# A GNN kernel's edge loop: block words loaded in the sixth step of a turn, with the addresses and waits of the next 27 matmuls computed ahead of the load

## The reference

```python
N, E, D, EF, L = (3125, 12500, 128, 16, 3)        # the inputs have 100,000 edges
s2, d2 = concatenate([src, dst]), concatenate([dst, src])
for l in range(L):
    e_in = concatenate([h_prev[s2], h_prev[d2], ef2], axis=-1)
    msg = leaky_relu(e_in @ We1[l]) @ We2[l]
    red = segment_sum(msg, d2, num_segments=N)
    n_in = concatenate([h_prev, red], axis=-1)
    out = leaky_relu(n_in @ Wn1[l]) @ Wn2[l]
    h_prev = out + h_prev
x = layernorm(x + out)
```

## The kernel before

| ahead of | step 0 | steps 1 and 2 | steps 3 to 11, each |
|---|---|---|---|
| tile 1 | 5 (38) | 3 (15) | 3 (15) |
| tile 2 | 3 (15) | 3 (15) | 3 (15) |
| tile 3 | 3 (13) | 3 (13) | 3 (13) |
| sums | 6 (33) | 6 (33) | 2 (12) |

## Time and profile before

### The profile page before, as it was taken

The page is one execution under the profiler, slowest core; times in us unless marked ns, Lnnn a source line. Parts: engine busy times, 40 slices in busy tenths (PEclk is TensorE's granted clock), DMA queues, the critical chain, the costliest instruction groups (busy, mean ns, idle before and its releaser), DMA issues.

```text
span 4538.9 us, 95215 instructions
## 1 busy us (share of the span) xinstructions
PE 3134.0 (69%) x28957; PEld 2255.1 (50%) x28958; DVE 2927.2 (64%) x7075; ACT 2092.5 (46%) x4052; POOL 780.5 (17%) x826
## 2 busy tenths in 40 slices
PE   3443443443442558888888879898888788988886
PEld 2111111111110556666666657777777577767774
DVE  7444444444443369999999966666666566666665
ACT  0000000000000346666666667777777677777774
POOL 0455555555555100000000000000000000000000
PEclk6555555555555779999999989999999899999998
DMA  6000000000000646666565624444444244444443
GB/s 176 4 5 5 5 5 5 5 5 5 5 5 5 147 123 212 207 213 209 207 215 204 214 102 162 162 154 163 153 159 157 86 164 152 164 152 159 157 155 112
DMA packets 191495, 533.07 MB, mean 117 GB/s; under 512 B 34359, under 2 KB 71958, under 8 KB 189430
## 3 DMA queue, kind: packets, MB, share of 16 engines
q1 hardware_dynamic: 163926, 517.51, 34.1%
q0 software_dynamic: 27552, 15.37, 1.8%
HBM read 375.40 MB, written 157.52 MB: 117 GB/s over the span
## 4 chain that ended last, share of the span: by engine, by line
PE 46%; DVE 10%; issue 9%; DMA 2%; ACT 1%; POOL 0%; DVEq 0%; SPq 0%; ACTq 0%; POOLq 0%
PE gath L1096 16%; PE sums L1151 12%; PE sums L1096 8%; PE gath L1089 5%; DVE loop_buf L875 3%; DVE loop_buf L892 2%; DVE big L806 2%; PE sums L1089 2%; DMA recc<-records 2%; PE sums L1001 1%; DVE gsel L810 1%; PE sums L1159 0%; PE sums L1021 0%; PE sums L1160 0%; PE sums L1165 0%
## 5 line engine op out<-in xcount | busy, mean ns | idle before, releaser
L806 DVE SCALAR_TENSOR_TENSOR big<-big 128x768 f32<-128x768 f32 (+1 forms) x957 | 907.7, 949 | 676.4 <-ACT big L593 635.0
L1096 PE MATMUL gath<-t_hi,gsel 128*128 x3744 | 944.9, 278 | 0.0
L1096 PE MATMUL gath<-t_lo,gsel 128*128 x3744 | 944.3, 278 | 0.0
L1151 PE MATMUL sums<-loop_buf 128*128 128x128 f16 x11232 | 793.7, 221 | 202.6 <-issue 202.0
L875 DVE TENSOR_TENSOR loop_buf<-big,loop_buf 128x768 f16<-128x768 f32 x936 | 889.7, 951 | 0.0
L507 POOL DMA_INDIRECT records<-rec,rowi x784 | 754.7, 963 | 630.7 <-DVE rec L747 391.2
L984 PE MATMUL sums<-t_lo,tri 128*128 128x326 f16 x784 | 345.5, 454 | 714.0 <-issue 480.2
L1151 PEld LDWEIGHTS sums<-loop_buf 128*128 128x128 f16 x11232 | 680.7, 99 | 311.0 <-issue 156.8
L725 DVE SCALAR_TENSOR_TENSOR gsel<-sums,t_lo 128x326 f32<-128x326 f32 x784 | 367.3, 496 | 724.0 <-remote 536.6
L597 ACT ACTIVATE loop_buf<-big 128x768 f16<-128x768 f32 x936 | 782.0, 836 | 1.9
L593 ACT ACTIVATE big<-gath 128x512 f32<-128x512 f32 x936 | 559.6, 598 | 356.8 <-PE gath L1096 356.8
(11 more groups left out here) (156 smaller groups left out, 2632.1 us busy)
## 6 DMA issues: line engine op xcount, KB each, us to landing
gsel<-gsel_d SPq DMA_DIRECT2D x208, 576.0 KB, 3.9
loop_buf<-ssel_d SPq DMA_DIRECT2D x208, 576.0 KB, 5.1
numb<-nums_d SPq DMA_DIRECT2D x106, 576.0 KB, 4.6
gsel_d<-gsel SPq DMA_DIRECT2D x104, 576.0 KB, 5.5
ssel_d<-loop_buf SPq DMA_DIRECT2D x104, 576.0 KB, 6.5
fchunk<-feat_d SPq DMA_DIRECT2D x313, 144.0 KB, 2.9
records<-rec,rowi POOLq DMA_INDIRECT x784
recc<-records POOLq DMA_DIRECT2D x30, 272.0 KB, 5.1
```

The source lines that it names most:

```text
L806: return dve.scalar_tensor_tensor(m, m, SLOPE, m, ALU.mult, ALU.max)
L1096: return pe.matmul(uv, gsel[:, h, (2 * tc + s) * P:(2 * tc + s + 1) * P], at[n], start=False, stop=n == 3, skip_group_check=True)
L1151: last = pe.matmul(out_n, m[:, place, w0:w0 + D], ssel[:, ts, s, :], start=False, stop=False, skip_group_check=True)
```

## The change

The load goes from the last step of a turn to the sixth (`q == LOAD_AT - 1`, `LOAD_AT` = 6). It now loads 16 words, those of steps 3 to 18 counted from the start of this turn, so up to step 6 of the next turn. Steps 0 to 5, and the gathers of step 6, use what the turn before has loaded; the rest of step 6 to step 11 uses what this turn loads. The load ahead of the loop fills the last ten registers. Each step takes its words with a snap of its own where it needs them (`word_of` is now a function), one for the gathers and one for the sums, instead of one snap of every register at the head of the turn. In step 5, ahead of the load, the addresses of its own 12 sum matmuls and the addresses and wait values of the 15 gather and feature matmuls of step 6 are worked out (`StepValues`), so that 27 matmuls can be issued behind the load with no register work between them. Matmuls, waits, operands and the other engines are unchanged.

```diff
--- before.py
+++ after.py
@@ -60,7 +60,9 @@
 BANK = 512
 BANKS = -(-NODES // BANK)
 AHEAD = 1
-WORDS = STEPS + LAG
+LOAD_AT = STEPS // 2
+WORDS = STEPS + LAG + 1
+FIRST_WORD = LOAD_AT - LAG
 BLOCK_BITS = 5
 assert NB <= 1 << BLOCK_BITS and STEP * 2 * BLOCK_BITS < 32
 SLOPE = 0.01
@@ -1037,17 +1039,19 @@
 
                     pe.reg_load(words, map_row[0:1, ds(first, WORDS)])
 
-                load_words(0)
+                pe.reg_load(words[STEPS - FIRST_WORD - LAG:], map_row[0:1, 0:WORDS - (STEPS - FIRST_WORD - LAG)])
                 with nc.Fori(0, TURNS, engines=(mybir.EngineType.PE,), hint_back_edge=True) as it:
                     with pe.If(it < live_n):
-                        word_of = [pe.snap(r) for r in words]
                         step0 = pe.snap(l * live_n * STEPS + it * STEPS)
                         turn = pe.snap((l * live_n + it) * PER_TURN)
 
-                        def places(t):
-
-                            q, i = divmod(t, STEP)
-                            word, nodes = word_of[q + LAG], []
+                        def word_of(step, before_load):
+
+                            return pe.snap(words[step - FIRST_WORD + (STEPS if before_load else 0)])
+
+                        def places(word, i):
+
+                            nodes = []
                             for k in (2 * i, 2 * i + 1):
                                 field = word // (1 << k * BLOCK_BITS) if k else word
                                 if k + 1 < 2 * STEP:
@@ -1061,17 +1065,17 @@
 
                             return t[:, plane * NODES:(plane + 2) * NODES].rearrange("p (k n) -> p k n", k=2)[:, :, ds(node0, P)]
 
-                        def gather_rows(t):
-
-                            lo, hi = places(t)
+                        def gather_rows(word, i):
+
+                            lo, hi = places(word, i)
                             at = rows(t_hi, lo, 0), rows(t_lo, lo, 0), rows(t_hi, hi, 1), rows(t_lo, hi, 1)
                             for ap in at:
                                 pe.lower_ap(ap)
                             return at
 
-                        def sum_places(t):
-
-                            lo, hi = places(t)
+                        def sum_places(word, i):
+
+                            lo, hi = places(word, i)
                             at = sums[:, ds(lo, P)], sums[:, ds(hi, P)]
                             for ap in at:
                                 pe.lower_ap(ap)
@@ -1096,6 +1100,26 @@
                             return pe.matmul(uv, gsel[:, h, (2 * tc + s) * P:(2 * tc + s + 1) * P], at[n], start=False,
                                              stop=n == 3, skip_group_check=True)
 
+                        class StepValues:
+
+                            def __init__(self, q):
+
+                                self.q = q
+                                self.word = word_of(q, q <= LOAD_AT)
+
+                            def tile(self, i):
+
+                                return gather_rows(self.word, i)
+
+                            def waits(self):
+
+                                q = self.q
+                                self.part_in = at_least(turn + upto(q // PART_STEPS)) if q % PART_STEPS == 0 else None
+                                self.x_free = at_least(step0 + (q + AHEAD))
+                                self.free6 = at_least(step0 + (q + 1))
+                                self.lo_in = at_least(step0 + (q + LO_AHEAD - LAG + 2))
+
+                        ready = None
                         for q in range(STEPS):
                             p = q // PART_STEPS
                             h = p % 2
@@ -1104,46 +1128,49 @@
                             uv6, uv7 = gath6, (gath[:, 0:2 * D], gath[:, 2 * D:4 * D])
 
 
-                            rows0 = gather_rows(t)
+                            now, rows_of = ready or (StepValues(q), None)
+                            if ready is None:
+                                now.waits()
+                            rows0 = rows_of[0] if rows_of else now.tile(0)
                             if first:
-                                part_in = at_least(turn + upto(p))
-                            x_free = at_least(step0 + (q + AHEAD))
-                            if first:
-                                pe.wait_ge(fchunk_in[h], part_in)
+                                pe.wait_ge(fchunk_in[h], now.part_in)
                             features(uv6, t, h, False)
                             if first:
-                                pe.wait_ge(gsel_set[h], part_in)
+                                pe.wait_ge(gsel_set[h], now.part_in)
                             for n in range(4):
                                 last = gather(uv6, rows0, t, h, n)
                             last.then_inc(gath6_done, 1)
 
 
-                            rows1 = gather_rows(t + 1)
-                            pe.wait_ge(x_set, x_free)
+                            rows1 = rows_of[1] if rows_of else now.tile(1)
+                            pe.wait_ge(x_set, now.x_free)
                             features(uv7[0], t + 1, h, True)
                             for n in range(4):
                                 gather(uv7[0], rows1, t + 1, h, n)
 
 
-                            rows2 = gather_rows(t + 2)
-                            free6 = at_least(step0 + (q + 1))
-                            lo_in = at_least(step0 + (q + LO_AHEAD - LAG + 2))
+                            rows2 = rows_of[2] if rows_of else now.tile(2)
                             if first:
-                                pe.wait_ge(ssel_set[1 - h], part_in)
+                                pe.wait_ge(ssel_set[1 - h], now.part_in)
                             features(uv7[1], t + 2, h, True)
-                            pe.wait_ge(mlo_set, lo_in)
+                            pe.wait_ge(mlo_set, now.lo_in)
                             for n in range(4):
                                 last = gather(uv7[1], rows2, t + 2, h, n)
                             last.then_inc(gath7_done, 1)
 
 
+                            of_sums = word_of(q - LAG, q < LOAD_AT)
+                            sum_at = [sum_places(of_sums, i) for i in range(STEP)]
+                            ready = None
+                            if q == LOAD_AT - 1:
+                                after = StepValues(q + 1)
+                                after.waits()
+                                ready = after, [after.tile(i) for i in range(STEP)]
+                                load_words(it * STEPS + FIRST_WORD + LAG)
+                            pe.wait_ge(gath6_free, now.free6)
                             place = (q - LAG) % RING
-                            sum_at = {t + i - STEP * LAG: sum_places(t + i - STEP * LAG) for i in range(STEP)}
-                            if q == STEPS - 1:
-                                load_words((it + 1) * STEPS)
-                            pe.wait_ge(gath6_free, free6)
                             for i in range(STEP):
-                                at_lo, at_hi = sum_at[t + i - STEP * LAG]
+                                at_lo, at_hi = sum_at[i]
                                 ts = (t + i - STEP * LAG) % SLOTS
                                 for s, out_n in ((1, at_hi), (0, at_lo)):
                                     w0 = i * 2 * D + (1 - s) * D
```

## The result

| | kernel before | kernel after |
|---|---|---|
| median (lowest to highest), us | 4537.26 (4534.35 to 4543.8) | 5414.4 (5409.38 to 5416.34) |
| profiled execution, its span, us | 4540.7, 4538.9 | 5413.0, 5411.3 |
| turn in pass 1 / 2 / 3, us | 36.58 / 33.63 / 33.67 | 47.82 / 44.87 / 44.96 |
| granted clock over the span | 0.806 | 0.792 |

The ratio of the times is 1.193, 95% interval 1.191 to 1.195: +877 us where +530 was forecast, and 234 us above the upper end of the range. A turn is here the mean distance of the first matmuls of step 0 of consecutive turns, over the 26 turns of a pass. The growth of the turns, 26 x 11.24 + 52 x 11.27, is 878 us, so practically all of it lies in the edge loop.

A forecast was written before the change was run, and what follows sets the result against it. PE's sequencer, working out addresses in registers, was taken as the bound nearly everywhere (DVE in pass 1). Turns of 41.3 us in passes 2 and 3 and 41.5 in pass 1 add 530 us: forecast 5067 us, range 4990 to 5180.

The forecast's parts named there:

- Unit price: Price of one register instruction on PE's sequencer, read at three places of the trace: 0.214 us.
- Words where they are used, +7.7 us a turn: Steps 3 to 11: sums' addresses worked out anew, 6 register instructions instead of 2, +7.7 us a turn.
- The rival of shared snaps: Builder shares equal snaps, so steps 3, 4, 5, 10, 11 keep 2 instructions; 4732 us, chance 0.05.
- Snaps, 0: Head of turn: 15 snaps go, 24 single ones come; between -0.4 and +0.4 us a turn, taken as 0.
- addresses ahead of the load, 0: Step 5: addresses and waits of 27 matmuls worked out before the load, same instructions in another order, price 0.
- back edge, 0: End of turn: branches stay, PE's gap shrinks but the sequencer's 2.0 us do not; price 0.
- The load's 1.5 us stay: Load moved from step 11 to step 5 still costs 1.5 us a turn; 16th word adds 0 to +0.1.
- The clock, 0 to +0.5: After the load, idle PE may drop to 1.2 GHz for the 27 matmuls: 0 to +0.5 us, caught up by step 9.
- Pass 1 at 41.5: Pass 1: PE becomes later than DVE, whose bursts hold it up a little; 41.5 us a turn, between 40.8 and 43.2.
- the sequencer has no lead: Rejects the faster rival: sequencer runs ahead of PE, hiding the load in passes 2 and 3; 4397 us, chance 0.05.
- the clock did not stay low: Rejects the rival that PE stays at 1.2 GHz, 56 us a turn; 6214 us, chance 0.03.
- the change did what it says: Rejects the no-change rival: extra addresses cancel against something in the order, within 0.2%; 4537 us, chance 0.01.

The follow-up runs named there:

- e12: Kernel after, but in steps 3, 4, 5, 9, 10 and 11 the sums reuse the word kept from the gathers three steps earlier; 4695.41 us (kernel before beside it 4194.14).
- e1: Kernel before with words taken by a snap of their own where used; load stays in step 11 with 15 words; 4813.51 us (kernel before beside it 4196.88).
- e2: Kernel after without the load in the loop, registers filled once ahead of a pass, most blocks wrong; 4611.89 us (kernel before beside it 4196.88).
- e10: Kernel before with a 16th word loaded into a spare register from the same place; 4150.23 us (kernel before beside it 4194.14).
- e9: Kernel before, its 15-word load beginning at 12 x turn + 6, blocks wrong; 4379.79 us (kernel before beside it 4194.14).
- e11: Kernel after, its load beginning at 12 x turn + 4 instead of + 6, blocks wrong; 4837.6 us (kernel before beside it 4194.14).
- e18: Kernel after with one-hot stores of pass 1 and their loads in passes 2 and 3 cut to one partition of 128; 5363.39 us (kernel before beside it 4564.57).
- v2: Kernel before with a 16-word load and fields cut by one remainder; 4034.76 us (kernel before beside it 4196.65), ratio 0.962.
- e6: Kernel after with the load put ahead of 13 of the 14 register instructions in step 5; 5419.81 us (kernel before beside it 4543.55).
- e8: Kernel after with the load behind the 6 register instructions for step 5's sums, ahead of the other 8; 5430.9 us (kernel before beside it 4543.55).
- e14: Kernel after with the load in the seventh step, first word 12 x turn + 7, ahead of the addresses; 5056.49 us (kernel before beside it 4196.65).
- e13: Kernel after with the load in the fourth step, first word 12 x turn + 4, blocks right; 4754.59 us (kernel before beside it 4196.65).
- e3: Kernel before without the load in the loop, four words used over and over, blocks wrong; 4073.51 us (kernel before beside it 4196.88).

## Why the prediction was wrong, point by point

- *What bounds the kernel* was right. Unit price: 0.214 us was read from before; e12's 24 instructions gave 0.21 each, after's 14 a step (the prediction counted 15) 3.15/14 = 0.225.
- *Words where they are used, +7.7 us a turn*: right. Steps of 3.21 were forecast, 3.15 came; e1, with this part alone, has turns of 41.76 in pass 2, +8.1, of which 0.3 is the load's. The rival of shared snaps was wrong; the sharing has to be written by hand (e12).
- *Snaps, 0*, *addresses ahead of the load, 0*, *back edge, 0*: the sum was right and its parts were not. After without the load (e2) has the turn forecast for it, 39.84 against 39.8. But the sums of steps 5, 6 and 7 come 4.67, 3.30 and 2.83 us apart, 10.8 for three steps that would take 9.4 at 3.12: computing ahead costs 1.4 us, since only part of what step 5 spends more comes back. The way from the sums of step 11 to those of step 1 is 7.19 and not 7.80, and the other steps' 3.12 for 3.21 make up the rest.
- ***The load's 1.5 us stay*: this step failed.** It carried a price measured at one place to another. I changed the words from 15 to 16 and the first word from 12 x turn to 12 x turn + 6 on paper, and priced only the first (+0.1; it is -0.5 by e10). The place costs 2.0 us for 15 words (e9 against before), 2.7 for 16 (after against e11). The hold was 4.0 us and not 1.5, each with the instruction for the load's address. By the Trainium skill (Runtime: NRT & Kernel Launch, Instruction fetch mechanics) a load takes about 200 ns a register even in bulk, an estimate of 3.2 us for 16. I had set it aside because before's 15 words took 1.5. It is near to what the misplaced load shows, 0.25 a word, and three times the 1.0 us of the aligned one (e10). The page's figure and the row differed by half, and I took the row as the truth of every load instead of asking what made it cheap.
- *The clock, 0 to +0.5*: at its upper end or above. PE stood still for 6 us, the 12 sums behind it took 1.46 us (1.2 GHz), and the turn is 5.03 us longer than without the load, of which 4.02 is the hold. The other 1.0 us is spread behind it, 0.75 of it in step 6 (4.05 against e2's 3.30), so that the term was about twice what I allowed.
- *Pass 1 at 41.5*: wrong on top, 47.82. Besides the 5.0 us, 2.6 come from the stores of one-hots that are issued just ahead of the load there (e18). The forecast looked at the queue of SP only for waits, and the load's new time had not been laid beside the transfers'.
- *The sum*: 52 x (44.9 - 41.3) + 26 x (47.8 - 41.5) = 351 us, which is the 347 between the forecast and the median. Of these some 195 are the load's hold (2.5 x 78 turns), some 80 what follows the low clock, and some 70 the stores in pass 1.
- *The rivals*: the sequencer has no lead (without its load, before's step 11 falls to the 2.35 of its neighbours, and the holds of 1 to 15 accesses show on PE in proportion), the clock did not stay low, and the change did what it says. None had a dearer load, so the range had no room for one. The signs named in the prediction were right but for three: the gap ahead of the sums of step 5 was 6.1 us and not 4, the turns 44.9 and 47.8 us and not 41, and turns of pass 1 differ by 3 us from the others, and not because of DVE (in e18, with DVE's work unchanged, they don't differ).

## What to carry to other kernels

A price read from a trace belongs to the operation with its operands. When a change moves an operation, ask what else of it changes, its first address and its length above all, and what transfers run at the new time; if one of these is new, the old price is only one end of the range. And where the sequencer bounds a loop, count its register instructions: 24 fewer by sharing gave back 5.0 us of a turn (e12), cheaper arithmetic with a 16th word made the kernel before 4% faster (v2), and computing ahead of the load cost 1.4 us a turn.

## What the runs showed of the hardware

- A load of words from on-chip memory into PE's registers fits accesses of 0.22 to 0.26 us, of four words where it begins on a multiple of 16 bytes and of one word elsewhere: 0.22 us for one word, 0.74 for 12, 1.00 for 16, but 1.48 for 15 and 3.45 for 15 that begin 8 bytes past such a multiple, each with the instruction for its address.
- In pass 1 such a load was held up by 2.4 to 3.2 us (after, e6, e8, e11, e12, e14, e1), 2.6 with 4 accesses (e11) as with 16 (after), where transfers that read the same on-chip memory are issued shortly before it begins or while it runs; with these cut the hold is gone (11.31 against 8.69 us, e18). Loads of one-hots, which write it, added nothing (e14, pass 2, 8.55 us), and nor, to 0.13 us, did stores that had been issued 4 us earlier and were still running (e13).
- A fused register instruction takes PE's sequencer 0.21 to 0.225 us, and PE has nothing in its queue to bridge such work in this loop (3.83 us with the load, 2.35 without, e3).
